# Source rows of the attention stack loads ordered by feature first, part second

## What is computed

```python
qkv = x @ qkv_w.T + qkv_b
q = apply_rope(q); k = apply_rope(k)
attn = jnp.einsum('bqhd,bkhd->bhqk', q, k) * scale
attn = jnp.where(mask[None, None], -1000000000.0, attn)
attn = jax.nn.softmax(attn, axis=-1)
out = jnp.einsum('bhqk,bkhd->bqhd', attn, v).reshape(B, S, D)
return out @ proj_w.T + proj_b
```

## Time and profile before

| | |
|---|---|
| median of 3 runs | 1332.59 us (1331.7 to 1334.64) |
| profiled execution, its own time | 1335.3 us |
| its span | 1333.5 us |
| mean granted clock of PE | 0.85 of 2.4 GHz |
| PE busy | 968.3 us (73%) |
| DVE busy | 624.2 us (47%) |
| ACT busy | 545.9 us (41%) |
| POOL busy | 290.1 us (22%) |
| DMA | 125.91 MB, mean 94 GB/s |

### The profile page before, as it was taken

The page is one execution under the profiler, slowest core; times in us unless marked ns, Lnnn a source line. Parts: engine busy times, 40 slices in busy tenths (PEclk is TensorE's granted clock), DMA queues, the critical chain, the costliest instruction groups (busy, mean ns, idle before and its releaser), DMA issues. The chain is left out here.

```text
span 1333.5 us, 24211 instructions
## 1 busy us (share of the span) xinstructions
PE 968.3 (73%) x6747; PEld 561.0 (42%) x6748; DVE 624.2 (47%) x1359; ACT 545.9 (41%) x1376; POOL 290.1 (22%) x480
## 2 busy tenths in 40 slices
PE   6599844458547745854684486398992799999997
PEld 3265411122112212211221122032782799999997
DVE  4275575257346634744563465260475233333332
ACT  3265511346335534633553364277253322223221
POOL 1265531122112201211220121032045011111111
PEclk9799955689678868977887797699796899999999
DMA  3244441210011001001100100310624566666662
GB/s 95 84 131 144 129 140 41 89 46 27 27 48 40 25 34 47 26 24 46 40 24 32 47 33 26 101 65 1 231 112 169 189 206 189 202 208 193 205 191 74
DMA packets 64545, 125.91 MB, mean 94 GB/s; under 512 B 9258, under 2 KB 42283, under 8 KB 58348
## 3 DMA queue, kind: packets, MB, share of 16 engines
q1 hardware_dynamic: 58908, 103.73, 24.3%
q0 software_dynamic: 5584, 21.54, 4.6%
HBM read 96.75 MB, written 28.48 MB: 94 GB/s over the span
## 5 line engine op out<-in xcount | busy, mean ns | idle before, releaser
L807 ACT ACTIVATE arena<-B_ps_s 128x512 f32<-128x512 f32 (+3 forms) x768 | 327.3, 492 | 414.4 <-PE B_ps_s L944 412.0
L866 DVE TENSOR_REDUCE B_block_max<-B_ps_item 128x8 f32<-128x1024 f32 x288 | 342.0, 1221 | 309.7 <-PE B_ps_item L929 307.8
L929 PE MATMUL B_ps_item<-k_stack,q_stack 64*128 64x128 bf16 (+3 forms) x1152 | 117.5, 298 | 279.0 <-DMA k_stack<-qk_parts 260.0
L944 PE MATMUL B_ps_s<-q_stack,k_stack 99*128 99x512 bf16 (+7 forms) x768 | 204.2, 353 | 3.8 <-ACT arena L807 3.1
L929 PEld LDWEIGHTS B_ps_item<-k_stack,q_stack 64*128 64x128 bf16 x1152 | 45.3, 97 | 347.5 <-issue 242.5
L960 PE MATMUL B_ps_o<-arena,B_v_quad 128*32 128x512 f32 (+3 forms) x1536 | 173.9, 526 | 1.0 <-ACT B_oacc L821 0.7
L1541 PE MATMUL D_ps_h<-D_xT,arena 128*128 128x128 f32 x1248 | 147.3, 277 | 2.1 <-ACT D_xT L1479 2.1
L1541 PEld LDWEIGHTS D_ps_h<-D_xT,arena 128*128 128x128 f32 x1248 | 146.7, 193 | 4.7 <-ACT D_xT L1479 2.8
L788 POOL TENSOR_SCALAR_AFFINE_SELECT arena<-arena 128x256 f32<-128x256 f32 x256 | 104.4, 408 | 202.6 <-ACT arena L807 200.3
L1560 PE MATMUL D_ps_y<-arena,D_hr 128*128 x624 | 141.0, 379 | 0.0
L944 PEld LDWEIGHTS B_ps_s<-q_stack,k_stack 99*128 99x128 bf16 (+1 forms) x768 | 55.5, 99 | 195.8 <-ACT arena L807 153.1
(11 more groups left out here) (142 smaller groups left out, 900.1 us busy)
## 6 DMA issues: line engine op xcount, KB each, us to landing
arena<-in_w_exp SPq DMA_DIRECT2D x39, 1024.0 KB, 4.9
qk_parts<-arena SPq DMA_DIRECT2D x64, 192.0 KB, 2.5
q_stack<-qk_parts SPq DMA_DIRECT2D x96, 128.0 KB
rows<-payload SPq DMA_DIRECT2D x39, 257.0 KB, 2.7
k_stack<-qk_parts SPq DMA_DIRECT2D x64, 128.0 KB
arena<-in_w_exp POOLq DMA_DIRECT2D x8, 1024.0 KB, 9.1
arena<-in_x SPq DMA_DIRECT2D x32, 128.0 KB, 2.6
k_stack<-qk_parts SPq DMA_DIRECT2D x64, 64.0 KB
```

The lines of the kernel that those rows point to most:

```text
L807: act.activation(pr[s % PR][:, h, 0:QW - off], ps_s[(QH * s + j) % R][:, 0:QW - off], ACT.Exp, scale=scale).then_inc(s_e, 1)
L866: dve.tensor_reduce(bmx[:, r, g:QH:GH, at:at + 4], src[:, :, :].rearrange("p c (b n) -> p c b n", n=P), AX.X, ALU.max).then_inc(s_free, 1)
L929: mm = pe.matmul(dst[:, half, at * P:(at + n) * P], qs[rows, r, half, bass.ds(g * SEQ + t * P, P)], ks[rows, r, half, bass.ds(g * SEQ + kb ...
L944: pe.matmul(ps_s[(QH * s + j) % R][:, 0:QW - off], ks[rows, r, half, bass.ds(g * SEQ + kb * P, P)], qs[rows, r, half, bass.ds(g * SEQ + c ...
```

## The change

In `load_stack` the order of the source rows changes. Where a DMA takes two parts (or one part twice) of 16 features, the part was the outermost dimension of the source and the feature the next; now the feature is outermost and the part the next. The target is the same block of 32 rows, so the rows of the two parts now alternate in it. k extra, which takes one part per DMA, is written to every second row, so that its rows meet those of q extra. Each product still has the same pairs, in another order of rows. The number, sizes and order of the instructions are the same on every engine.

```diff
             if step in steps:
                 sp.dma_start(qs[main + 2 * HD * p:main + 2 * HD * (p + 1), r, half, :],
-                             rows_of(0, p, half).rearrange("a (d g) n -> (a d) (g n)", g=GH).unsqueeze(0)
-                             .to_broadcast([2, HD, GH * SEQ])).then_inc(s_stk[r], 16)
+                             rows_of(0, p, half).rearrange("a (d g) n -> (a d) (g n)", g=GH).unsqueeze(1)
+                             .to_broadcast([HD, 2, GH * SEQ])).then_inc(s_stk[r], 16)
             step += 1
             if step in steps:
                 sp.dma_start(ks[main + 2 * HD * p:main + 2 * HD * (p + 1), r, half, :],
-                             rows_of(1, slice(0, 2), half).rearrange("j a (d g) n -> j (a d) (g n)", g=GH)).then_inc(s_stk[r], 16)
+                             rows_of(1, slice(0, 2), half).rearrange("j a (d g) n -> (a d) j (g n)", g=GH)).then_inc(s_stk[r], 16)
             step += 1
         if step in steps:
             sp.dma_start(qs[extra:extra + 2 * HD, r, half, :],
-                         rows_of(0, slice(0, 3, 2), half).rearrange("j a (d g) n -> j (a d) (g n)", g=GH)).then_inc(s_stk[r], 16)
+                         rows_of(0, slice(0, 3, 2), half).rearrange("j a (d g) n -> (a d) j (g n)", g=GH)).then_inc(s_stk[r], 16)
         step += 1
         for p in range(2):
             if step in steps:
-                sp.dma_start(ks[extra + HD * p:extra + HD * (p + 1), r, half, :],
+                sp.dma_start(ks[extra + p:extra + p + 2 * HD - 1:2, r, half, :],
                              rows_of(1, 2 - 2 * p, half).rearrange("a (d g) n -> (a d) (g n)", g=GH)).then_inc(s_stk[r], 16)
```

## The result

The changed kernel takes 1034.74 us (median of 4 runs, 1032.45 to 1037.15) against 1332.14 (4 runs); the ratio is 0.7766, with a 95% interval from 0.7745 to 0.7788. Forecast were 1048 us and a range from 1034 to 1092: the result lies in the range, 0.7 us above its low end, and the gain of 297 us is 13 more than the 284 forecast. The profiled execution took 1037.15 us, with a span of 1035.4.

The account below looks back on a forecast made before the run. PE waiting for stack loads, mostly on two DMA engines, was taken as the bound. Load -260, projection -10 and period start -15 sum to -285 us: 1335.3 gives 1050.3, less 2.7 is 1048 us; range 1034 to 1092.

Parts of the forecast that it names:

- What bounds the kernel: Attention: PE stands about 17 us of each 46 us period for a stack load, ten of whose 14 DMAs use two engines.
- The load: -260.0 us: Attention's stack load takes 10.7 us in place of 29.8 and is hidden, so all 15 PE waits go: -260.0 us.
- the cover: Second half of an attention period: the 12.7 us from a load's first issue until PE needs it; forecast margin 2.0 us.
- The projection: -10 us: Projection: the first item's load no longer delays the x loads, so 12 tiles take 45.0 us, not 55.3; -10 us.
- The start of a period: -15 us: Attention: without the stall PE's clock is not low at a period's start, 1.0 us for each of 15 periods; -15 us.
- the bound of 1.9 us: Period start: most that could be gained per period, as if all of the first 4 us ran at twice the clock.
- The lag of ACT: Period start: ACT ends 1.1 us after PE; if PE must wait that out, a period gets 1.1 us longer.
- The short cover: Rival: attention's load still lands late, with stalls of 1 to 4 us per period, 1063 to 1108 us; chance 0.22.
- The half rate on 32 rows: Stack load: 32 target rows reach only part of the memory's ways, 208 GB/s, data 7.6 us; one way to a late load.
- ACT or DVE as the bound: Rival: in attention the 1.1 us backlog stays each period and the fast start is lost, 1080 us; chance 0.07.
- no effect: Rival: the load's dimensions are folded or re-ordered before descriptors are made, so time stays 1332.6 us; chance 0.05.
- pieces too small: Rival: load rows are cut into small pieces, slower under about 96 bytes, 1553 us at 64 bytes; chance 0.02.

Follow-up runs that it names:

- single2: Kernel before, but each stack load is 24 one-part DMAs of 64 KB, features outermost, ordered so that the outermost source dimension has size two; 1390.03 us.
- single4: Kernel before, but each stack load is 24 one-part DMAs of 64 KB, features outermost, ordered so that the outermost source dimension has size four; 1199.39 us.
- more_issues: Changed kernel with each q main DMA cut in two, one per copy, to every second row: 18 DMAs per load in place of 14; 1067.83 us.
- extra_ahead: main_only with both q extra DMAs of a load issued first, in front of the loop over the halves; 1078.41 us.
- warm_before: Kernel before with 72 extra PE products put before the wait for the stack load, in all periods but the first; 1368.77 us.
- main_only: Changed kernel with the two q extra DMAs of a load back to parts outermost and k extra back to rows in a run; 1104.55 us.

## Why the prediction was right, and where it was off

*What bounds the kernel.* Right: two engines for ten DMAs of fourteen. The row that carried it was the window with nothing else under way, a share of 0.13 at 52 GB/s; single2 and single4 reproduce it at will.

*The load: -260.0 us.* Right in the sum, all 15 waits are gone. Off in its working: an issue was taken at 0.39 us, from 16-row and x loads, and measured 0.57 for the two-part DMAs and 0.54 for L251. That more rows cost no issue was wrong here: 16 rows cost 0.37 and 32 rows of the same sixteen features 0.57, and every second row as target 0.17 more than a run. So the load takes 11.6 us and not 10.7, and its margin is 1.0 us and not 2.0. It didn't show in the time only because the cover just held; that part is luck.

*The projection: -10 us.* Right: -9.9 in the trace; with the old first load the projection ends 9.5 us later again (162.91 against 153.45), and the kernel takes 8.9 us more.

*The start of a period: -15 us.* Right in the mechanism, too small by half, and this is where the missing 13 us are. There are two errors. I had counted two of the operations in the slow stretch (0.64 + 0.36 = 1.0 us) and left out the block products and two more scores there; the period that I had read, from 395.06, loses 1.5 us (28.57 to 27.07). And it was the shortest of the 13, which have 29.3 us on the mean. Windows over the first part of it and of the next one (the kernel before, columns as in the earlier trace rows):

```profile
395.06:411.00 15.94, 15.94 (x104) 4.12 (x104) 12.14 (x12) 10.50 (x25) 4.06 (x11) 0.90 0.01 3
```

```profile
440.75:456.70 15.95, 15.95 (x100) 4.00 (x100) 11.08 (x11) 9.97 (x23) 3.63 (x10) 0.83 0.01 2
```

The clock is at the lower level until 398.3 in the one and until 446.1 in the other, 3.2 us and 5.3 us from the start. So the bound of 1.9 us, which went by 4 us at the lower level, was too small as well. Measured are 2.2 us per period (29.3 to 27.07), 29.9 in all. With it the sum is 260.0 + 9.8 + 29.9 = 299.7, and 1.6 came back in route and ffn, which I can't tell from the spread of the runs. The range's low end rested on the 1.9 too, so that the result lies inside it, by 0.7 us, is in part luck. The lag of ACT, my reason for a loss of 1.1, cost nothing.

*The rivals.* The short cover didn't come, but was 1.0 us away; more_issues has it, at 1067.8, in that rival's range. The half rate on 32 rows did not come as such: an engine moves 26 GB/s when two work and 16 to 18 in the windows above, when all work on these loads. But it is slower with other targets too: 302 GB/s at 0.94 are 20 GB/s per engine, and so it is in the ffn of the kernel before, where most of the traffic is 1 MB weight loads (206 GB/s at 0.66, again 20):

```profile
1107.00:1114.00 7.00, 7.00 (x50) 6.59 (x49) 2.37 (x9) 2.04 (x7) 0.98 (x1) 1.00 0.66 206
```

By the Trainium skill (SBUF — State Buffer, "Door 1: The DMA port swizzle") 32 partitions from 0 on reach 8 of 16 ports, with 218 GB/s as the asymptote. The highest window of the changed kernel's load, 191 GB/s, stays under it; extra_ahead has 229 from 452 to 454, with loads to more than one block of 32 rows under way. No run here separates the ports from other causes. ACT or DVE as the bound, no effect, and pieces too small did not come. The page does show more packets:

```profile
DMA packets 66785, 125.92 MB, mean 122 GB/s; under 512 B 11498, under 2 KB 44523, under 8 KB 60588
```

That is 2240 more than the 64545 before, all of them under 512 B (9258 before), and 2240 is 14 for each of the 160 DMAs that went from two engines to sixteen. The rows themselves were not cut up, since the packets of 512 B and more are as many as before (55287).

## What to carry to other kernels

In the kernels here, and as a first guess in others: look at the DMA share while nothing but one load runs: n/16 with a queue that fills says that the DMAs run on n engines, and the outermost dimension of source and target is the thing to change, not the number or size of the DMAs. A few such DMAs left among good ones still cost (two of fourteen cost 70 us here): all the others need their engines too. When a stall is removed, count the slow clock after it as part of the stall, over everything that runs in that stretch, and on the mean of several periods.

## What the runs showed of the hardware that I had not expected

- The issue of a DMA on SP costs 0.63 to 0.67 us on two or four engines, 0.37 with 16 rows on sixteen, 0.56 to 0.58 with 32 rows on sixteen, and 0.54 with 16 rows to every second row of the target. Once the data are fast, this price is the length of a load.
- One DMA engine moved 26 GB/s when two were at work and 21 with four (80 GB/s at a share of 0.24). With all at work it moved 16 to 18 in the busiest windows of the stack loads (14 to 21 over the windows of one load of the changed kernel), and 20 in the ffn, mostly on 1 MB weight loads. These are the GB/s of a window over its share of 16 engines.
- How PE's granted clock took a short wait differed from period to period. After waits of 1.2 to 1.6 us it stayed at the upper level over nine of ten periods of more_issues and four of ten of warm_before. After 1.8 to 2.7 us (extra_ahead) and 2.6 to 4.0 us (main_only) it was at the lower level for a part of each of 12 periods, although ten of the 12 in extra_ahead and two in main_only start with a product at the upper one.
